# Layer 0's first sequence in buffer sets 1 and 2 instead of 2 and 1, and new places for the side work of the first turns

## What is computed

```
skip = norm1(x) * (1 + scale) + shift
z    = norm2(skip) Wz + bz ;   act = silu(norm2(skip) Wx + bx)
for direction s in (forward, backward over time):
    u     = z Wc_s + bc_s                              # 512 channels
    delta = softplus((u Wdbc_s)[:64] Wdt_s + bdt_s);   B, C = 16 states each, from u Wdbc_s
    h[t]  = exp(delta[t] A) h[t-1] + delta[t] B[t] u[t]
    y_s   = sum over states of h C + u D
out = x + gate * ((act * (y_0 + y_1)) Wf + bf + skip)
```

## Time and profile before

| | us |
|---|---|
| median of 3 runs | 3290.21 |
| profiled execution, its own time | 3297.11 |
| its span, first to last instruction | 3295.4 |
| TensorE busy (matmuls) | 3022.8 |
| ScalarE busy | 2818.3 |
| VectorE busy | 2678.8 |
| GpSimd busy | 2655.1 |

### The profile page before, as it was taken

The page is one execution under the profiler, slowest core; times in us unless marked ns, Lnnn a source line. Parts: engine busy times, 40 slices in busy tenths (PEclk is TensorE's granted clock), DMA queues, the critical chain, the costliest instruction groups (busy, mean ns, idle before and its releaser), DMA issues.

```text
span 3295.4 us, 63649 instructions
## 1 busy us (share of the span) xinstructions
PE 3022.8 (92%) x21772; PEld 2525.4 (77%) x21772; DVE 2678.8 (81%) x3433; ACT 2818.3 (86%) x6502; POOL 2655.1 (81%) x3086
## 2 busy tenths in 40 slices
PE   6778789999999999999999999999999999988896
PEld 3667677778787888888788887878788887876764
DVE  1667788979798988979898998979798997968762
ACT  2768878899999999999999999998999989887843
POOL 0787999889898898988898898989898897868730
PEclk8899999999999999999999999999999999999998
DMA  5121222222222222222222221222222222212100
GB/s 201 55 76 53 73 79 72 78 67 83 69 81 73 71 84 65 85 67 84 67 81 73 68 86 65 85 67 85 67 74 81 68 82 60 72 52 68 57 25 9
DMA packets 133872, 239.57 MB, mean 73 GB/s; under 512 B 15374, under 2 KB 31054, under 8 KB 133296
## 3 DMA queue, kind: packets, MB, share of 16 engines
q1 hardware_dynamic: 133552, 235.50, 23.3%
HBM read 230.36 MB, written 5.08 MB: 71 GB/s over the span
## 4 chain that ended last, share of the span: by engine, by line
PE 55%; ACT 21%; DVE 10%; POOL 7%; issue 5%; DVEq 0%; POOLq 0%; ACTq 0%
PE ps_b L710 12%; PE ps_v L738 12%; ACT decay L777 8%; DVE hst L818 5%; POOL g L833 5%; PE ps_v L917 5%; ACT dbut L788 4%; PE ps_x L923 3%; PE ps_x L1449 3%; PE ps_x L1476 3%; PE ps_v L968 3%; PE ps_v L923 2%; PE ps_x L917 2%; POOL dbut L798 2%; ACT L874 2%
## 5 line engine op out<-in xcount | busy, mean ns | idle before, releaser
L833 POOL TENSOR_TENSOR g<-hst,c_bc 128x512 f32<-128x512 f32 x1536 | 1975.6, 1286 | 428.4 <-PE ps_v L738 394.1
L818 DVE TENSOR_TENSOR_SCAN hst<-decay,ps_b 128x512 f32<-128x512 f32 x1536 | 1821.5, 1209 | 317.1 <-PE ps_b L710 170.6
L777 ACT ACTIVATE decay<-delta,acoef 128x256 f32<-128x256 f32 x3072 | 1379.2, 499 | 26.8 <-DVE hst L818 25.9
L710 PE MATMUL ps_b<-ident,dbut 128*128 128x128 f32 x6144 | 943.0, 277 | 150.2 <-DVE hst L818 65.9
L738 PE MATMUL ps_v<-ident,g 128*128 128x128 f32 x6144 | 941.7, 276 | 13.9 <-ACT u L1130 12.1
L710 PEld LDWEIGHTS ps_b<-ident,dbut 128*128 128x128 f32 x6144 | 706.9, 142 | 231.1 <-issue 138.8
L738 PEld LDWEIGHTS ps_v<-ident,g 128*128 128x128 f32 x6144 | 727.5, 142 | 143.9 <-issue 67.8
L798 POOL TENSOR_SCALAR dbut<-dut,bcm 128x256 f32<-128x256 f32 x1536 | 750.2, 489 | 79.9 <-ACT dut L1029 79.9
L788 ACT ACTIVATE dbut<-dut,bcm 128x256 f32<-128x256 f32 x1536 | 767.9, 501 | 31.5 <-PE ps_b L710 28.9
L1561 DVE TENSOR_REDUCE mxt<-ps_x 128x4 f32<-128x1024 f32 x120 | 144.6, 1205 | 10.1 <-PE ps_x L1449 10.1
L1532 ACT ACTIVATE pT<-ps_x 128x1024 f32<-128x1024 f32 x120 | 121.8, 1015 | 30.3 <-PE ps_x L1487 25.7
(11 more groups left out here) (264 smaller groups left out, 3614.9 us busy)
## 6 DMA issues: line engine op xcount, KB each, us to landing
c_bc<-c_rows SPq DMA_DIRECT2D x768, 256.0 KB, 3.1
weights<-in_weights_dram SPq DMA_DIRECT2D x1, 4320.0 KB, 24.3
x<-in_x_dram SPq DMA_DIRECT2D x16, 256.0 KB, 4.0
rows_bc<-mod_rows SPq DMA_DIRECT2D x16, 256.0 KB, 3.9
gate<-mod_rows SPq DMA_DIRECT2D x32, 128.0 KB, 3.6
out_dram<-x SPq DMA_DIRECT2D x16, 256.0 KB, 3.5
wc<-in_wc_dram SPq DMA_DIRECT2D x1, 2048.0 KB, 11.2
maskrow<-mask_rows SPq DMA_DIRECT2D x16, 128.0 KB, 3.3
```

Of the source, the lines that this page charges most:

```text
L710: last = nc.tensor.matmul(ps_b[:, u % 2, e * T + t * P:e * T + (t + 1) * P], dbut[:, u % NDBU, t, e * P:(e + 1) * P], ident[:, :], is_tran ...
L777: last = nc.scalar.activation(decay[:, u % (DA_AHEAD + 2), e, :], delta[slot(b, s)][:, eb, :], ACT.Exp, scale=acoef[:, s, eb, n:n + 1])
L818: nc.vector.tensor_tensor_scan(line(hst[:, u % NHST, :, :].rearrange("p e t -> p (e t)")), line(decay[:, u % (DA_AHEAD + 2), :, :].rearran ...
L833: nc.gpsimd.tensor_tensor(g[:, u % NG, :, :], hst[:, u % NHST, :, :], c_bc[:, k % NCB * CHUNK + n % CHUNK, :].unsqueeze(1) .broadcast_to([ ...
```

## The change

Sequence 0 uses set 1 for direction 0 and set 2 for direction 1 (slot). The waits that guard the sets follow. In the first three stages many places are new; all of ada (twelve pieces on TensorE) goes to place 22 of stage 0, and prep1 of sequence 1 has its first four pieces on TensorE at 62 to 64 and its last four at 106.1 to 107.

```diff
--- before.py
+++ after.py
@@ -186,63 +186,63 @@
             "SP": (-15, 31),
         },
         "prep0": {
-            "PE": (0, 0, 107, 107, 107, 107, 107, 107),
+            "PE": (0, 0, 106.1, 106.2, 106.3, 106.4, 106.5, 106.6),
             "ACT": (107, 107, 107, 107, 107, 107, 107, 107, 107, 107),
             "DVE": (107, 107, 107),
             "SP": (107, 107),
         },
         "prep1": {
-            "PE": (111, 112, 122.091, 122.273, 122.455, 122.818, 122.909, 123),
-            "ACT": (122, 122.071, 122.143, 122.214, 122.357, 122.429, 122.714, 122.786, 122.857, 123),
-            "DVE": (123, 123, 123),
-            "SP": (119, 121),
+            "PE": (106.9, 107, 112, 115, 118, 120, 120.25, 120.75),
+            "ACT": (112, 115, 115.5, 115.75, 119, 119, 122, 122, 122, 123),
+            "DVE": (118, 118.333, 119),
+            "SP": (112.667, 113),
         },
         "l0_mx": {
-            "PE": (122.182, 122.364, 122.545, 122.636, 122.727),
-            "ACT": (122.286, 122.5, 122.571),
+            "PE": (106.7, 106.8, 111.333, 111.667, 114.5),
+            "ACT": (111.5, 114.5, 115.25),
         },
     },
     0: {
         "l0_in": {
-            "PE": (12, 14, 14, 17, 17, 20, 20, 22, 22, 36),
-            "ACT": (10.643, 10.929, 14, 17, 21, 23, 35),
-            "DVE": (-5, 13, 13),
-            "SP": (-5, 1),
+            "PE": (8, 8.5, 9, 11, 11, 13, 13, 15, 15, 35),
+            "ACT": (4, 7, 10, 12, 14, 16, 34),
+            "DVE": (-5, 6, 6.667),
+            "SP": (-5, 0.333),
         },
         "prep0": {
-            "PE": (36, 36, 38, 39, 42, 46, 47, 49),
-            "ACT": (37, 39, 41, 41, 44, 44, 48, 48, 48, 50),
-            "DVE": (42, 45, 46),
+            "PE": (35, 35, 37, 38, 41, 45, 46, 47.5),
+            "ACT": (36, 37, 39, 39, 43, 43, 46, 46, 47, 48),
+            "DVE": (41, 44, 45),
             "SP": (37, 39),
         },
         "prep1": {
-            "PE": (63, 63, 65, 106.136, 106.409, 106.727, 106.909, 107),
-            "ACT": (64, 106, 106.083, 106.167, 106.333, 106.417, 106.667, 106.75, 106.833, 107),
-            "DVE": (106.333, 106.5, 106.833),
+            "PE": (62, 63, 64, 64, 106.111, 106.556, 106.889, 107),
+            "ACT": (64, 64, 64, 64, 106.2, 106.4, 106.6, 106.7, 106.8, 106.9),
+            "DVE": (94.5, 106.5, 106.75),
             "SP": (97, 97),
         },
         "l0_mx": {
-            "PE": (106.318, 106.364, 106.5, 106.545, 106.682),
-            "ACT": (106.25, 106.5, 114),
+            "PE": (99, 99, 101, 101, 103),
+            "ACT": (102, 104, 114),
         },
         "l0_post": {
-            "PE": (62, 64, 95, 96, 97, 106.045, 106.091, 106.273),
-            "DVE": (95, 95, 106.167),
+            "PE": (48, 49, 95, 96, 96, 96, 96, 99),
+            "DVE": (49, 95, 98),
         },
         "ada": {
-            "PE": (64, 65, 94.5, 106.182, 106.227, 106.455, 106.591, 106.636, 106.773, 106.818, 106.864, 106.955),
-            "DVE": (111,),
+            "PE": (22, 22, 22, 22, 22, 22, 22, 22, 22, 22, 22, 22),
+            "DVE": (24,),
         },
     },
     1: {
         "l0_in": {
-            "PE": (12, 14, 14, 15.25, 15.5, 20, 20, 36, 36, 37.5),
-            "ACT": (10.583, 10.917, 13, 15, 21, 33.5, 36.333),
-            "DVE": (10.667, 11, 12),
-            "SP": (13, 13),
+            "PE": (10.222, 10.333, 10.444, 10.667, 10.778, 20, 20, 35.333, 35.667, 36.5),
+            "ACT": (8, 10.1, 10.3, 10.5, 20, 33.5, 36.333),
+            "DVE": (6, 8, 10.25),
+            "SP": (3, 5),
         },
         "prep0": {
-            "PE": (44, 44, 49, 50, 53, 57, 59, 60),
+            "PE": (47, 47, 49, 50, 53, 57, 59, 60),
             "ACT": (48, 50, 52, 52, 55, 55, 59, 59, 59, 61),
             "DVE": (53, 56, 57),
             "SP": (47, 49),
@@ -258,18 +258,18 @@
             "ACT": (71.333, 73.5, 114),
         },
         "l0_post": {
-            "PE": (38, 39, 66, 67, 67, 67, 67, 69),
+            "PE": (37, 39, 66, 67, 67, 67, 67, 69),
             "DVE": (38.5, 67, 68.667),
         },
         "l1_in": {
-            "PE": (15.75, 16, 18, 18, 23, 23, 28, 28, 29, 29, 33),
-            "ACT": (17, 19, 21, 26, 31, 32),
-            "DVE": (15, 17, 17, 20, 20, 21, 22, 25, 25, 26, 27),
+            "PE": (14, 14, 17, 17, 23, 23, 28, 28, 29, 29, 33),
+            "ACT": (11, 16, 19, 26, 31, 32),
+            "DVE": (11, 13, 13, 20, 20, 21, 22, 25, 25, 26, 27),
         },
         "prep2": {
-            "PE": (33, 33, 35, 36, 37, 41, 43, 44),
-            "ACT": (33, 34, 36, 36, 36.667, 37, 41, 41, 41, 43),
-            "DVE": (38, 39, 40),
+            "PE": (33, 33, 35, 36, 40, 44, 45, 47),
+            "ACT": (33, 34, 36.667, 37, 41, 41, 43, 43, 45, 46),
+            "DVE": (39, 43, 43),
             "SP": (35, 37),
         },
         "ada": {
@@ -603,8 +603,8 @@
 
         def slot(b, s):
 
-            if s == 0 and b == 0:
-                return 2
+            if s < 2 and b == 0:
+                return s + 1
             return 0 if s == 2 and b == LAST - 1 else s
 
         def du_of(b, s):
@@ -987,8 +987,8 @@
             yield next(at)
             act.wait_ge(S[f"dbc_full_{s}"], nth(f"dbc_full_{s}", b, 1))
             if s == 0:
-                after(act, b - 1, "dt_full_1", 2)
-                after(act, b - 1, "c_stored_1", 16)
+                after(act, b - 1, "dt_full_1" if b > 1 else "dt_full_0", 2)
+                after(act, b - 1, "c_stored_1" if b > 1 else "c_stored_0", 16)
             if s == 2 and b < LAST - 1:
                 after(act, b - 3, "y3_full", 1)
             elif s == 2:
@@ -998,8 +998,8 @@
                 after(act, b, "dt_full_0", 2)
                 after(act, b, "c_stored_0", 16)
             if s == 2 and b == 0:
-                after(act, b, "dt_full_0", 2)
-                after(act, b, "c_stored_0", 16)
+                after(act, b, "dt_full_1", 2)
+                after(act, b, "c_stored_1", 16)
             nc.scalar.activation(dbc[i][:, :], bk[0:DBC, 0:T], ACT.Identity,
                                  bias=dbcb[:, s:s + 1]).then_inc(S[f"dbc_sb_{s}"], 1)
             yield next(at)
@@ -1124,7 +1124,7 @@
                 yield next(at)
                 act.wait_ge(S["z_full"], nth("z_full", b, k + 1))
                 if b >= 1 and (b, k % 2) != (1, 0):
-                    act.wait_ge(S["u_added"], scans.added[b - 1, k % 2, k // 2])
+                    act.wait_ge(S["u_added"], scans.added[b - 1, k % 2 if b > 1 else 0, k // 2])
                 for j in range(2):
                     eb = 2 * (k // 2) + j
                     last = nc.scalar.activation(u_s[slot(b, k % 2)][:, eb, :], bank(ps_v, A, 2)[:, j, :], ACT.Identity,
```

## The result

The changed kernel takes 3300.56 us (median of 20 runs, 3290.36 to 3305.48) against 3290.53 for the kernel before (20 runs). The ratio is 1.0026, with an interval of 1.0018 to 1.0034: 8.6 us slower by the ratio, just inside the 0.3% that the prediction called no change, and 4.6 us above its 3296. By the two medians it is 10.0 us, and the median itself lies 0.5 us above the 3300.1 at which the prediction's "no change" ended: the result stands on that border.

What follows compares the result with a forecast made beforehand. The prediction took GpSimd's pace as the floor, 27.2 us per 16 units; 3297.11 + 3 + 13 + 0 - 10 + 0 = 3303 for the profiled execution, which lies 6.9 above the median, so median 3296; range 3280 to 3309.

Steps and rivals of the forecast that it cites:

- Start of the first scan, +4: Before the first unit: ten more TensorE instructions at 1.2 GHz, 4.75 us, taken as 4 us of delay.
- First group with its start, +3: First 16 units with their start: spread preparation sums to 43.1 us against 40.48, so 3 us slower; bounds -4 and +8.
- the wait for TensorE's turns: First group, ticks 121 to 123: turns wait for ScalarE's scaling and copies, about 4.5 us, 1.9 covered, so 2.6.
- ada, +13: Second group: twelve pieces at tick 22, six fast and six slow, 15.4 us, 13 net; bounds 8 and 17.
- Third and fourth group, 0: These groups and the seam: nothing shortened, the 4.87 us du and its stall stay; 0, bounds -2 and +2.
- Fifth and sixth group, -10: Lump's GpSimd idle 8 instead of 17.05, -9; work behind it -5.5; +4 ahead; together -10, bounds -16 and -3.
- "+4" for output matmuls and l0_mx: Fifth group, ticks 96 to 103: half the output matmuls and l0_mx now lie there, costing 4 us.
- Later, 0: Later groups: same work under the same engines despite shifted places; 0, bounds -3 and +3.
- Rival 1: Clock stays 2.4 GHz: ada costs 8, first group's spread gains 4, fifth group gains 16; median 3278, chance 0.20.
- Rival 2: First group: du of sequence 0's direction 1 collides with GpSimd, 3.65 us more; median 3300, chance 0.15.
- Rival 3: Fifth group: the lump keeps its length, -3 instead of -10; median 3303, chance 0.12.
- rival 4: Whole kernel: the moves cancel and only order changes; 3290, chance 0.08.

Runs made afterwards that it cites:

- e1: Changed kernel with ada's twelve pieces spread over places 18 to 57 and VectorE's part at 59: 3288.63 us, 0.9992 of the kernel before.
- e3: Changed kernel with ada's matmuls given 64 moving columns instead of 16, same place and instructions: 3293.42 us, 1.0001 of the kernel before.
- e6: Changed kernel with ada's pieces spread over 18 to 57 and VectorE's part at 66, in the drain: 3286.99 us, 0.9984 of the kernel before.
- e8: Changed kernel with VectorE's modulation of sequence 2 moved from place 8 into the lump (10.1): 3302.47 us, 1.0040 of the kernel before.
- e10: Changed kernel with ada spread, VectorE's part at 66, and output pieces and l0_mx one a tick from 96: 3284.59 us, 0.9981 of the kernel before.
- e2: Kernel before with only ada moved, all twelve pieces at tick 22: 3303.93 us, 1.0035 of the kernel before.
- e9: Kernel before with only ada moved, pieces spread over 18 to 57 and VectorE's part at 66: 3293.28 us, 1.0008 of the kernel before.
- e5: Kernel before with only the buffer sets and their waits changed, every place as before: 3288.27 us, 0.9995 of the kernel before.
- e4: Changed kernel with the old places of prep0, prep1 and l0_mx of sequence 0 restored: 3311.36 us, 1.0051 of the kernel before.
- e7: Changed kernel with sequence 0's four output-matmul pieces one a tick from 96 and l0_mx later: 3298.35 us, 1.0024 of the kernel before.

## Why the prediction was right, and where its terms were off

The sign, the size and the main cause were right: 3296 forecast, 3300.56 measured, with a range from 3280 to 3309. By terms:

- **Start of the first scan, +4.** Measured +3.7 in this execution. In e1, e3, e6, e8 and e10, which have the same places there, the first scan came 4.9 to 5.4 us after the end of prep0, against 6.4 here and 2.6 before: +2.2 to +2.7.
- **First group with its start, +3.** Measured 0: 43.06 us from the end of prep0 to unit 16, 43.05 before (41.0 to 41.6 in the five runs just named). ScalarE was busy 33.4 us of the 36.7 after the first scan, for 34.5 in the working, and idle 3.25 for 4.6. Of these, 2.28 are the 2 us put on VectorE:

```profile
107.90 1.21 DVE L1049 TENSOR_TENSOR pT<-delta,u 128x1024 f32<-128x1024 f32 x1
...
110.64 0.91 ACT L777 ACTIVATE decay<-delta,acoef 128x256 f32<-128x256 f32 x2 [2.28 <-DVE hst L818]
```

  The two longest gaps, of 7.46 and 4.59 us between scans 6 to 8, are mostly of VectorE's making: 8.6 us of its side work (delta, modulation, statistics, du) stand in them. The term that was too large is the wait for TensorE's turns, 1.0 for 2.6.
- **ada, +13.** Measured +16.4. The mechanism held (e1, e2, e3). The mis-sized term is the share of slow pieces and what one takes: six of twelve were taken at 1.63, nine and a half were slow (76 of the 95 steps from one instruction to the next took 0.21 us, 19 took 0.11) at 1.7, and the run lasted 18.5 us instead of 15.4. The share depends on the moment at which the clock falls, which differs between executions (e3).
- **Third and fourth group, 0.** Measured -2.9. du of sequence 1 took its short form, 1.55 us; the sum had said that the 4.87 stays. Its new place, one tick earlier, is not needed for that: in e2, with the old place, it took 1.53, and in e9 1.51, but 4.88 in e5.

```profile
192.67 1.55 DVE L1049 TENSOR_TENSOR pT<-delta,u 128x1024 f32<-128x1024 f32 x1
```

- **Fifth and sixth group, -10.** Measured -6.4. The lump is right: 8.21 us of idle GpSimd for a forecast of 8. The "+4" for output matmuls and l0_mx before it was too small: units 64 to 75 took 26.5 us instead of 17.4, +9.1, of which VectorE's modulation at tick 104 (a gap of 6.13) was not in the working at all. It had counted TensorE's work there and left out a move of VectorE's. Of the rest, 1.5 is the clock in the output block: the gap at unit 66 is 7.40 here and 5.87 in e3, e4 and e8, where the block ran at 2.4 GHz.
- **Later, 0.** +1.3 up to unit 272 and +1.1 from there to the last scan, inside its bounds. The sixth du took 5.32 us for 1.68 before.

The sum was 6.0 against 9.6 between the ends of the profiled executions; ada's 3.4 and the fifth group's 3.6 too little are partly made up by the first, third and fourth group, on which the working was too high; that the total came so close is in part this luck. Rival 1 (the clock stays high in ada's run and in the first group) is refuted by the trace. e3 shows what the first of its three terms would have given, 7.3 us where 5 were put on it; the other two, together 13, were not tested. Rival 2: sequence 0's du took 1.21 us, since GpSimd stood idle beside it, from 107.84 to 110.74; its mechanism showed up elsewhere (e1). Rival 3 did not happen. Of rival 4 something is true: with ada at 22 in both kernels the edit's other parts cancel, to 3 us by the ratios (e2 against the change), which these runs don't tell from none. With ada spread in both they do not cancel (e6 against e9).

## What to carry to other kernels

Work that fills an engine's wait is free only there: nine of ada's pieces sat under another chain without making it longer, at the price of some 5 us of slow turns behind it (e2, e9), and all twelve in one place of an undisturbed stretch cost 16.4 us. When pieces are moved into a paced stretch, set them apart by as much as the slack per unit covers, and ask of each move what it does on every engine, VectorE's small operations included. Freeing a buffer earlier is worth nothing until something in the written order uses it.

## What the runs showed of the hardware

- In a run of matmuls with 16 moving columns, with TensorE busy throughout, the granted clock fell from 2.4 to 1.2 GHz after 2.0 to 4.6 us (five executions); the same run with 64 columns stayed at 2.4 GHz and took 10.9 us instead of 18.5 (one execution). Nine narrow pieces among other work, one every second unit, left the clock at 1.00 (e1).
- VectorE operations with two SBUF inputs can take far longer beside a GpSimd that works without a pause: 0.18 us became 1.80 for 128x32 (e1), 0.48 became 1.39 for 128x256, and du of the same shape took 1.2 to 5.3 us. Which form comes is not settled by an operation's place alone (du of sequence 1 in e2, e5 and e9), and what decides it these runs don't show. Groups that no edit touched moved by up to 4 us between kernels (the eleventh group took 35.3 us in eight of twelve, 31.4 in e4 and e7).
